# Attention features in row tiles, weights split and folded, a search on two engines, expert gathers issued earlier

## What is computed

```python
# block 1: linear attention with random features (16 heads of 16, 64 features), then a ReLU layer
q, k, v = split(x @ Wq.T + bq), split(x @ Wk.T + bk), split(x @ Wv.T + bv)
xp   = (x * norm) @ proj.T                       # features of q and of k
diag = sum(x**2) * 0.5 * norm**2
qp = ratio * (exp(xp_q - diag_q - max over the row) + 1e-4)
kp = ratio * (exp(xp_k - diag_k - max over all tokens and features of the head) + 1e-4)
out = (qp @ (kp.T @ v)) / (qp @ sum of kp over the tokens)
x2 = layer_norm(video + out @ Wo.T + bo, g2, be2)
x  = layer_norm(x2 + relu(x2 @ W1.T + b1) @ W2.T + b2, g3, be3)
# block 2: 8 experts, each takes the 512 tokens (of 4096) that its gate scores highest
scores = softmax(xf @ gate_w.T)                  # 4096 x 8
vals, idx = top_k(scores.T, 512)                 # per expert
y = layernorm(xf[idx]) * ln_w + ln_b
out = (gelu(y @ fc1.T + b1) @ fc2.T + b2) * vals
xf = xf.at[idx].add(out)
```

## Time and profile before

| what | value |
|---|---|
| median of 3 runs (lowest, highest) | 1084.2 us (1073.0, 1085.6) |
| span of the profiled execution | 1083.8 us |
| the profiled execution's own time, beside its span | not listed apart; the median stands 0.4 us above the span |
| PE busy / DVE / ACT / POOL | 822.4 / 739.8 / 389.7 / 419.6 us |
| chain that ended last | PE 46%, DVE 26%, issue 13%, POOL 5%, DMA 5%, ACT 4% |
| mean granted TensorE clock | 0.883 |

### The profile page before, as it was taken

How to read it: one execution, slowest core, us unless ns; L and a number is a source line. 1 busy time by engine, 2 the same in 40 slices (tenths; PEclk the granted TensorE clock), 3 DMA queues, 4 the chain that set the end, 5 groups by cost and what they waited for, 6 DMA issues and landing times.

```text
span 1083.8 us, 13642 instructions
## 1 busy us (share of the span) xinstructions
PE 822.4 (76%) x4637; PEld 617.3 (57%) x4637; DVE 739.8 (68%) x1594; ACT 389.7 (36%) x578; POOL 419.6 (39%) x339
## 2 busy tenths in 40 slices
PE   5669899899799889889879895911123998899920
PEld 3246665675666666666556574710112888888820
DVE  1747538858958868768777767568894665666635
ACT  1444623623624624623532541200001543344314
POOL 3151503624523515425333344321053344454237
PEclk9889999999989989989989997955555999999975
DMA  6000010011001011011011011123003365555155
GB/s 200 1 20 1 1 39 1 20 40 40 20 21 59 0 39 59 0 39 59 0 39 40 1 41 39 40 79 104 0 0 121 105 179 158 152 152 136 26 153 177
DMA packets 60599, 64.95 MB, mean 60 GB/s; under 512 B 7952, under 2 KB 57232, under 8 KB 60560
## 3 DMA queue, kind: packets, MB, share of 16 engines
q1 hardware_dynamic: 53584, 55.63, 16.0%
q0 software_dynamic: 6144, 8.52, 4.5%
q10 hardware_dynamic: 832, 0.30, 0.1%
HBM read 43.33 MB, written 21.10 MB: 59 GB/s over the span
## 4 chain that ended last, share of the span: by engine, by line
PE 46%; DVE 26%; issue 13%; POOL 5%; DMA 5%; ACT 4%; POOLq 0%; DVEq 0%; ACTq 0%; SPq 0%
PE pF L1340 7%; PE pX L1540 6%; PE pF L1304 5%; PE pA L1290 4%; PE pX L1311 4%; DVE z L808 4%; PE pX L1275 4%; PE pA L1297 3%; DMA xg<-row_scratch,idx_g 3%; PE pA L1350 3%; DVE st L798 3%; DVE qe L1036 2%; PE pA L1275 2%; POOL xg L730 2%; PE pX L1304 2%
## 5 line engine op out<-in xcount | busy, mean ns | idle before, releaser
L1340 PE MATMUL pF<-w,h 128*128 128x256 f32 x512 | 114.8, 380 | 0.0
L1340 PEld LDWEIGHTS pF<-w,h 128*128 128x128 f32 x512 | 96.1, 190 | 18.6 <-issue 5.9
L738 POOL DMA_INDIRECT acc_scratch<-at,idx_s x32 | 53.4, 1668 | 105.4 <-DVE at L1138 98.7
L658 POOL TENSOR_SCALAR ve<-mv 128x4 f32<-128x4 f32 x48 | 11.1, 231 | 188.1 <-DVE mv L802 173.4
L1304 PE MATMUL pF<-x2T_hi,w_lo 128*128 128x512 f32 x128 | 64.5, 504 | 23.5 <-ACT h L450 22.1
L564 ACT ACTIVATE h<-pX,b1cur 128x512 f32<-128x512 f32 x64 | 44.0, 690 | 98.7 <-DVE b1cur L1149 63.0
L1540 PE MATMUL pX<-w_lo,h_hi 128*128 128x256 f32 x256 | 74.3, 290 | 0.8 <-issue 0.8
L1540 PE MATMUL pX<-w_hi,h_lo 128*128 128x256 f32 x256 | 73.4, 287 | 0.0
L1540 PE MATMUL pX<-w_hi,h_hi 128*128 128x256 f32 x256 | 73.3, 286 | 0.0
L1311 PE MATMUL pX<-projbd,qT 128*128 128x512 f32 x128 | 62.0, 609 | 8.1 <-DVE qe L856 8.1
L1121 DVE TENSOR_TENSOR h_lo<-h,h_hi 128x512 fp32r<-128x512 f32 x64 | 42.9, 690 | 27.0 <-ACT h_hi L556 24.1
(11 more groups left out here) (236 smaller groups left out, 2167.3 us busy)
## 6 DMA issues: line engine op xcount, KB each, us to landing
kp<-fc1T SPq DMA_DIRECT2D x8, 1024.0 KB
w<-fc2T SPq DMA_DIRECT2D x8, 1024.0 KB
xin<-video SPq DMA_DIRECT2D x8, 512.0 KB, 3.7
x<-video SPq DMA_DIRECT2D x8, 512.0 KB, 4.6
x_scratch<-x SPq DMA_DIRECT2D x8, 512.0 KB, 3.0
acc_scratch<-xf SPq DMA_DIRECT2D x8, 512.0 KB, 2.9
row_scratch<-y SPq DMA_DIRECT2D x8, 512.0 KB, 3.0
qp<-x_scratch SPq DMA_DIRECT2D x2, 1024.0 KB
```

What stands on the lines that cost most here:

```text
L738: pool.indirect_dma_start(acc_d, bass.IndirectOffsetOnAxis(ap=idx_s[:, g:g + 1], axis=0), og[:, g, :], None, compute_op=ALU.add).then_inc( ...
L1340: ins = nc.tensor.matmul(slots[m][:, half * D:(half + 1) * D], h[:, k, tok(2 * m + half)], w2[:, k, :], start=(k == 0), stop=(k == FC - 1))
```

## The change

- **Projections.** Wq, Wk, Wv, Wo and their inputs are split in float32r halves (`by_halves`, and `by_tokens` with six parts instead of two). ACT copies the high halves, DVE subtracts the low ones (`rest_of_x`, `rest_of_heads`, `rest_of_weight`).
- **Features of k and q** (`features`): each matmul takes 32 rows (two heads) and 128 columns, four row tiles side by side that write to four banks of PSUM. 64 matmuls per batch instead of 16.
- **q in feature order** (`features_turned`): only the maxima are taken in token order (`q_max`), turned (`turn_tops`), and then projection, sum of squares and maximum are added in PSUM by three row-tiled matmul sets that come out in feature order already. ACT's exponential (`exp_q`) writes `qp` straight from PSUM. `q_sub`, `turn_q` and the additions of 1e-4 to q are gone; 1e-4 times the context's sums becomes a bias (`sums_of_context`).
- **Maximum of k**: a transpose, a reduction and a small matmul (`turn_kmax`, `k_top`, `spread_kmax`) instead of `partition_all_reduce`; all four subtractions on DVE.
- **Folded weights**: g2 is multiplied into W1, be2's product into b1, bv's product into bo; ln_w and ln_b are applied after the gathers by ACT; the norm of the gathered rows is derived from that of x1 (`root_rows`, `normed_rows` on ACT), so one statistics pass and POOL's affine of y are gone. x2's g2 and be2 move to POOL.
- **Search**: 4 of 7 counts on DVE, 3 on ACT (Sign with an accumulated sum); the rounds are unrolled, and the high and the low bits are searched as two numbers.
- **Indices**: one-hots laid out with the innermost step 1, four groups instead of eight, the product with the token number on DVE.
- **Gates**: 32 columns instead of 128, in column tiles, then one transpose.
- **Experts**: `gather(e + 2)` is issued before all scatters of e, and DVE prepares its indices right after the last `h_lo`.

```diff
-            def features(i, n, src, t):
-
-                s = slot_x(i, n)
-                for g in range(G):
-                    ins = nc.tensor.matmul(s[:, g, :], src[:, g, tok(t)], projbd[:], start=True, stop=True)
+            def features(i, n, src, half):
+
+                slot_x(i, n)
+                for t2 in range(2):
+                    for g in range(G):
+                        cols = tok(2 * t2 + g)
+                        for a in range(4):
+                            rows = slice(32 * a, 32 * a + 32)
+                            ins = nc.tensor.matmul(pXall[:, a, cols], src[rows, g, tok(2 * half + t2)], projbd[rows, :], start=True, stop=True,
+                                                   tile_position=(32 * a, 0))
                 ins.then_inc(x_ready, 1)
...
-                def turn_q(n):
-
-                    s = slot_x(i, J_TQ + n)
-                    for k in range(2):
-                        for t in range(TT):
-                            ins = turn(s[:, k, tok(t)], qe[:, t, tok(2 * n + k)])
+                def features_turned(g):
+
+                    slot_x(i, J_QT + g)
+                    if g == 0:
+                        pe.wait_ge(qsq_ready, i + 1)
+                    for n, (w_, x_) in enumerate(((projbd[:], qT[:, g, :]), (selc[:].rearrange("p k m -> p (k m)"), qsqT[:, g, :]),
+                                                  (selm[:, g].rearrange("p k m -> p (k m)"), mxT))):
+                        for a in range(4):
+                            rows = slice(32 * a, 32 * a + 32)
+                            ins = nc.tensor.matmul(pXall[:, a, :], w_[rows], x_[rows], start=(n == 0), stop=(n == 2), tile_position=(32 * a, 0))
...
-                    pool.wait_ge(kmax_ready, i + 1)
-                    settled(pool)
-                    nc.gpsimd.partition_all_reduce(stabk[:], kmax[:], P, RMAX).then_inc(stab_ready, 1)
-
-                    pool.wait_ge(kbias_ready, i + 1)
-                    for t in (TT - 2, TT - 1):
-                        kt = kp[:, t, :].rearrange("p (h m) -> p h m", m=M)
-                        nc.gpsimd.tensor_tensor(kt, kt, kbias[:, t, :].unsqueeze(2).to_broadcast([P, H, M]), ALU.subtract).then_inc(ksp_ready, 1)
...
+            def k_top(i, steps):
+
+                dve.wait_ge(a_ready, i * A_JOBS + J_ST + 1)
+                steps.link(nc.vector.tensor_reduce(smax[:], pA[J_ST % 2][0:H, 0:P], AX_X, ALU.max))
+                nc.vector.tensor_scalar(sdiag[:], ident[0:H, 0:H], smax[:, 0:1], None, ALU.mult).then_inc(stab_ready, 1)
...
             def expert(e, after):
 
+                if after == 2:
+                    gather(e + 2)
                 wait(pool, scattered, e * 16 * GT)
                 pool.wait_ge(idxs_ready, e + 1)
-                scatter(e, range(GT // 2))
-                if after == 2:
-                    gather(e + 2)
-                scatter(e, range(GT // 2, GT))
+                scatter(e)
```

ACT's new part of the search, and its new order in a body:

```diff
+            for rd in range(ROUNDS):
+
+                act.wait_ge(s_ready, 1 if rd < HI_ROUNDS else 3)
+                act.wait_ge(cand_ready, rd + 1 if rd < HI_ROUNDS else rd)
+                now = cand_low if rd == HI_ROUNDS else cand
+                for j in range(CANDS - CANDS_V):
+                    k = CANDS_V + j
+                    nc.scalar.activation(signs[:, j], S_top if rd < HI_ROUNDS else S, ACT.Sign, bias=now[:, k:k + 1], scale=-1.0,
+                                         accum_out=cnt[:, k:k + 1]).then_inc(sgn_ready, 1)
...
+                    exp_q(i, 0)
+                    exp_q(i, 1)
+                    cs_copy(i, 0)
+                    cs_copy(i, 1)
+                if ut:
+                    normed_rows(u)
```

More of the change, by code:

```diff
@@ L731, in gather, with scatter @@
                                             ).then_inc(gathered, 16)
-            def scatter(e, tiles):
-                for g in tiles:
+            def scatter(e):
+                for g in range(GT):
                     pool.wait_ge(og_ready, e * GT + g + 1)
@@ L888, in body @@
                         nc.vector.tensor_tensor(z[:], z[:], over_tiles(be3_b), ALU.add).then_inc(za_ready, 1)
+                if f is not None:
+                    for c in range(C):
+                        dve.wait_ge(x2T_ready, f * C + c + 1)
+                        nc.vector.tensor_tensor(x2T_lo[:, c, :], pF[c][:], x2T_hi[:, c, :].bitcast(F32), ALU.subtract).then_inc(x2l_ready, 1)
                 if i is not None:
@@ new lines, in body @@
+                    hidden(1)
+                if att:
+                    features(i, J_XK + 1, kT, 1)
+                    pe.wait_ge(qT_ready, (i + 1) * G)
+                    if isinstance(i, int) and i == 0:
+                        pe.wait_ge(wqkvo_in, 16 * 4)
+                        pe.wait_ge(proj_ready, 2)
+                        for c in range(C):
+                            ins = nc.tensor.matmul(pF[1][:, 0:D], bv_wide[:, c], wo[:, c, :], start=(c == 0), stop=(c == C - 1))
+                        ins.then_inc(fold_ready, 1)
@@ new lines, in body @@
+                if ff:
+                    hidden(2)
+                    hidden(3)
+                if att:
+                    features(i, J_XQ, qT, 0)
+                if ff:
+                    hidden(4)
+                    hidden(5)
+                if att:
+                    turn_kmax()
+                if ff:
+                    hidden(6)
+                if att:
+                    features(i, J_XQ + 1, qT, 1)
+                    spread_kmax()
+                    if isinstance(i, int) and i == 0:
+                        pe.wait_ge(w1_in, 16)
+                        pe.wait_ge(wff_in, 16 * N_WFF)
+                        for n in range(FC):
+                            for c in range(C):
+                                ins = nc.tensor.matmul(pF[0][:, n:n + 1], w1_raw[:, c, tok(n)], be2_c[:, c:c + 1], start=(c == 0), stop=(c == C - 1))
+                        ins.then_inc(fold_ready, 1)
@@ L1416, in body @@
+                if ff:
+                    hidden(7)
                 slots = [None, None]
                 if ff:
-                    for half in range(2):
-                        ff_out(0, slots, half)
+                    ff_out(0, slots, 0)
                 if att:
+                    turn_tops()
+                if ff:
+                    ff_out(0, slots, 1)
+                if att:
+                    features_turned(0)
                     pe.wait_ge(kp_ready, (i + 1) * TT)
```

759 lines of the change are left out of this document (428 added, 331 removed).

## The result

The changed kernel takes 907.9 us, median of 4 runs (903.4 to 908.4), against 1080.4 (1073.0 to 1085.6) for the kernel before: a ratio of 0.841, 95% interval 0.836 to 0.846. The forecast was 950 with a range from 890 to 1010. The profiled execution spans 906.5 us against 1083.8, 177.3 less where 134 were forecast. The forecast's own range, 925 to 975 with a chance of 0.55, missed it; the outer range from 890 to 1010 holds it.

A forecast was written before the change was run, and what follows sets the result against it. A batch was taken as bound by PE's stream plus a chain DVE, POOL, DVE. From 1083.8: batches -101, setup +2, draining bodies -13, search -7, index lists -4, experts -11 give 950 us; own range 925 to 975, outer 890 to 1010.

The forecast's parts named there:

- its cause lies 30 us earlier: Loop batch: PE's 5.29 us wait before q's third turn was put down to POOL's late maximum of k.
- a second matter: Loop batch: DVE's normalization of z takes 7.68 us while POOL adds kp; the two engines hold one another up.
- The tile term: Row-tiled features of k and q per batch: 128 short records at 8.1 us, 4.7 more than perfect tiles.
- so I take 0.063: Features of k and q: 0.063 us per short row-tiled record, taken from the 16 column-tiled records of the sums.
- some 19 us less: Row-tiled matmuls: at the skill's 3.07 times gain a batch takes 69 us, the total some 19 less than forecast.
- What the prediction feared: Row-tiled matmuls: each short one brings a 32-row weight load as long as one of 128, speaking against the change.
- The walk: One loop body stepped through with new orders and old durations, assuming four row tiles overlap; next batch starts at 66.3 us.
- The folding: Batch 0: folding g2, be2 and bv on PE, DVE and POOL, covered by some 25 us; up to 10 if uncovered.
- that case: Index lists: one-hots at two elements per cycle through step 1 take 10.4 us, making the total 8 less.
- the tail: Search: the part of a round beyond its seven counts, 1.7 us, kept the same after the change.
- Perfect tiles: Rival, chance 0.18: features at 3.4 us, hand-overs as walked, 66 a batch, one-hots at double rate; 901 us.
- that rival: Slower rival, chance 0.04: row tiles do not overlap at all, a batch some 92 us, total 1117 us.

The follow-up runs named there:

- both waits out: Kernel before with POOL's library maximum of k made a plain copy and POOL's three kp sums cut to 16 columns: 1023.7 us.
- the run with a broadcast: Changed kernel with the one-hots' digits compared against a row of numbers whose last step is a broadcast, not step 1: 914.5 us.
- the later normed rows: Changed kernel with ACT's four normed rows moved behind its copies of the attention's output and the turned xf: 902.1 us, ratio 0.844 to the kernel before.

## Why the prediction was right in direction and too high

- **What bounds a batch.** PE's stream of 72 us was right (72.6 busy with both waits out). Of the 13 us that the prediction called waits 9.0 are idle time of PE; the other 4 are the stream at a low granted clock (76.3 busy, with a mean clock of 0.94 in the loop). The cause that the prediction gave for the longest, "its cause lies 30 us earlier" in POOL's maximum of k, was wrong: without the library instruction it stays at 5.2. It came from DVE's 7.68 us beside POOL's sums, which the prediction named as a second matter. The chain of waits showed a gap on POOL, and I joined it to the longest wait of PE without following DVE's queue: the instruction that PE waited for stood right behind z's normalization, an addition and two statistics and one more addition.
- **The tile term.** The step that failed most is "so I take 0.063". The row it came from, 16 records in 1.01 us, ran at a granted clock of 0.50, as the windows above show. At full clock those records take 0.58, 0.036 each, and the changed kernel's features 0.034. So of the 4.7 us added per batch 3.7 were this error (8.1 counted, 4.4 measured), and the turned features came 0.4 dearer than perfect tiles. The trace disagrees with the rule of 3.07 times (the Trainium skill, TensorE: Matmul & The Clock Gate, Part 3): 512 columns in four tiles go at 0.107 us a record, a quarter of the 0.43 that one takes. The prediction's "some 19 us less" by that rule should read 17 (8 x 2.1). The same page's section LDWEIGHTS (loading the stationary operand) has a load of 32 rows as long as one of 128; the trace agrees, 186 ns against 188 to 190. What the prediction feared from it did not come, since the features, with a load each, start 0.034 apart. Whether the loads are why they run 3.4 times and not four times as fast, no run shows.
- **The walk.** The walk puts the batch at 66.3, 5.3 of them waits beside a stream of 61; measured are 62.3 busy and 2.5 idle, so waits were taken 2.8 too long. It had PE's third column tile waiting 1.5 for ACT behind the normed rows; that wait exists, 0.8.
- **Batch 0: forecast 59, measured 65.6.** The folding was costed at nothing, with batch 1's hidden parts as the place where it is due. They did wait for nothing. But the cost lay where the work runs: 7.0 us of PE's stream for 32 records of one column, and POOL's passes over W1, beside which DVE's four rows of the next batch took 8.4 us instead of 1.4. With both moved out of the way batch 0 takes 59.5, the forecast's number; 0.6 of the 6.1 us come from the later normed rows, and how the rest splits is open.
- **Search: forecast -7, measured -13.5.** The mis-sized term is ACT's count, put at 0.7: it takes 0.49 from start to start, so ACT's three are done before DVE's four, and a round takes 3.16 us instead of 3.8. And the tail was kept at 1.7 us plus 1 us once for the join; it is 1.56.
- **Index lists: forecast -4, measured -11.5.** I took the row's rate of one column per cycle and named the other as a rule beside it. The Trainium skill, VectorE: DVE Perf Modes, the tier table, gives a tensor_tensor on 16-bit data in SBUF twice the plain rate; the trace agrees, 0.60 us for 1024 against 1.2, and the run with a broadcast shows that it hangs on the step. The one-hots take 9.4 us in all where 18.9 were counted (the prediction's 10.4 for that case was 1 too high), so the 8 us that it gave for that case are the miss.
- **Experts, draining bodies, last stage.** -11 forecast and -11.9 measured; -13 and -11.6; 0 and 0.
- **The rivals.** "Perfect tiles", 901, with chance 0.18, is nearest, within 7 us, and its sign is there, starts 0.03 apart. That the total comes so close is in part luck: this rival has the batches at 505 us, measured are 518, and the search, for which it has no gain of its own, gives back 6.5. Without overlap the kernel would have been slower, as that rival said, and by more than its price.

## What to carry to other kernels

Read the granted clock of the stretch beside every duration that you take as a rate: right behind the 5.3 us wait it was half, and the row from there made the new work look nearly twice as dear. Where PE waits, follow the queue of the engine that it waits for back to the last long instruction before you blame a gap further up, and test it by shortening that one. Small row tiles pay in full only if neighbours in PE's order lie in different row groups: 1.10, 2.75 and 3.8 us for the same 32 records with the groups changing at each matmul, group after group, and all in one group.

## What the runs showed of the hardware

- With one row group of 32 in use, the granted clock fell to 0.50 while PE's rows show it busy without a gap; with four groups in turn and neighbours in different groups it stayed at 1.00. It stayed at 1.00 also where the groups came one after another and overlapped in part, so no run tells whether the unused rows or the missing overlap brought it down.
- DVE's `tensor_scalar` on f32 in SBUF, 4 x 256 columns, takes 1.4 us alone, 7.7 beside POOL's additions and 8.4 beside POOL's scaling and splitting of W1. The Trainium skill, SBUF — State Buffer, SBUF: two separate sides, tells of an exclusive lock on a port pair that the two engines share; the trace agrees: in the earlier trace rows POOL's last sum ends at 463.7 and DVE's four instructions at 463.8.
- A wait of PE costs more than its length, by the low clock behind it: the 5.3 us one was followed by 4.6 us at 0.50 and cost 7.8, and taking 2.05 us a batch off the other gave 3.4.
